# A memset behind each early gather, replaced by a wait for the gather two in front

## The chip, the cores and the metric

The kernel runs on one core of a Trainium2 chip. Its time is the device time of one execution, in microseconds; of the kernel before there are three runs, and their median is 1738.09 us (1730.94 to 1742.48). One further execution was taken with the hardware profiler, and all rows below are of that one.

A core has five engines with one instruction stream each: TensorE (PE, its weight loads PEld), VectorE (DVE), ScalarE (ACT), GpSimd (POOL) and SyncE (SP). They meet only at semaphores. Sixteen DMA engines move data; SP and POOL each feed a queue of their own.

## The reference

One layer of message passing on a graph with 100000 nodes of 64 numbers and 25000 edges:

```python
h = relu(layernorm(x))
edge_in_f = concat(h[src], h[dst], edge_attr)
edge_in_r = concat(h[dst], h[src], edge_attr)
agg = segment_sum(mlp_f(edge_in_f), dst) + segment_sum(mlp_r(edge_in_r), src)
out = x + h + mlp_n(concat(agg, h))
```

Each `mlp` is two matrix products with a relu between them; messages have 128 numbers. All is in 32-bit floats.

## The kernel before, in words

Three passes follow each other.

*First node pass.* The nodes go in 98 windows of 1024. SP loads a window of x (L384), DVE and ACT normalise it, PE multiplies it by the part of the first node weights that meets h, and SP stores the rows, 512 KB a window, to a table in memory (L390). Helper functions whose names end in `begin` are this pass.

*Edge pass.* The edges go in 98 batches of 256, two to a pair, so 49 pairs. For each batch the rows of x at both ends of its edges are needed: four tiles of 128 rows of 64 numbers, each fetched by an indirect DMA that POOL issues (L505, a "gather": 128 rows of 256 bytes, 32 KB). They are normalised, multiplied, and the messages of equal targets are joined; POOL then adds them to the table with four indirect DMAs (L523, a "scatter"). A batch's scatters wait for the landing of the batch before (L514 or L516). Behind such waits stands `sem_inc`, which counts up a semaphore that nobody waits for; wait and count are one instruction of POOL's own sequencer, and the indirect DMA behind it is another.

*Second node pass.* The table is read back, window by window, the node network is finished, and the result is stored.

**The early gathers.** The rows for the even batches of all 49 pairs are fetched during the first node pass into `got_even`, 196 gathers (4 per pair); those of the odd batches of the first four pairs into `got_odd`, 16 gathers. The other odd gathers, 180, are issued later, between the scatters. The early ones stand on POOL in a plain sequence, after a short setup: for each of the first four pairs four odd and four even, then only even ones. The first of all waits for the row numbers (`s_first`, counted up by DVE at L876); it carries that wait itself. Behind each even gather stands a memset of a tile that nothing reads (`idle`, 128 x 512, L550), which waits for the memset before it. All even gathers count up one semaphore, `s_got_even`, by 16 each when they land.

DVE waits for all of them at once (L1063) after the first node pass; its next instruction (L1066) and all of the edge pass on DVE stand behind that wait. POOL's scatters stand behind the last early gather.

Of the kernel before, what the change touches and what calls it, by code (L numbers as in the profile page):

```python
# [28 lines left out]
P = 128  # L29
# [31 lines left out]
def run(eng, count, loops, behind, body):  # L61


    done = 0
    for begin, end, unroll in loops:
        assert begin % unroll == 0 and end % unroll == 0
        for n in range(done, begin):
            body(Step(count, n))
        with eng.Fori(0, (end - begin) // unroll) as turn:
            turn = eng.snap(turn)  # L70
            for n in range(unroll):
                body(Step(count, n, begin, unroll, turn))
        done = end
    for n in range(done, count + behind):
        body(Step(count, n))


def gnn_layer(nc, x, src, dst, edge_attr, W1_f, b1_f, W2_f, b2_f, W1_r, b1_r, W2_r, b2_r, Wn1, bn1, Wn2, bn2, out):
# [7 lines left out]
    KB = 2 * JT  # L86
    NT = -(-E // (P * JT)) * JT
    NB = NT // JT
    PAIRS = NB // 2
    TB = NT // 2  # L90
    TAIL = E - (NT - 1) * P
    RING = 4
    assert NB % 2 == 0 and 0 < TAIL < P and TB < P

    SPARE = N
# [20 lines left out]
    with ExitStack() as ctx:  # L116
        def sb(name, shape, dt=F32):
            return ctx.enter_context(nc.sbuf_tensor(name, shape, dt))

        def sem(name):  # L120
            return ctx.enter_context(nc.semaphore(name))

        def sems(name):
            return [sem(f"{name}{s}") for s in range(2)]
# [30 lines left out]
        def two(name, shape, dt=F32):  # L155
            return [sb(f"{name}{s}", [P] + shape, dt) for s in range(2)]
# [4 lines left out]
        gather_first = sb("gather_first", [P, NB * KB], I32)  # L161
        gather_at = [sb(f"gather_at{p}", [P, KB], I32) for p in range(RING)]
        got_even = sb("got_even", [P, PAIRS, KB * D])
        got_odd = [sb(f"got_odd{p}", [P, 1, KB * D]) for p in range(RING)]
        sums = two("sums", [KB])
# [28 lines left out]
        nstd = two("nstd", [G])  # L194
        nh = [sb(f"nh{p}", [P, G, D]) for p in range(NRING)]
        nxh = [sb(f"nxh{p}", [P, G, D]) for p in range(NRING - 1)]
        idle = sb("idle", [P, 512])
        kept_more = sb("kept_more", [P, MORE, G * D])
        nturned = two("nturned", [G // 2 * P])
        nhidden = two("nhidden", [G * P])  # L200
# [19 lines left out]
        s_others = sems("others_in_")  # L220
        s_gat = [sem(f"gather_at_ready{p}") for p in range(RING)]
        s_got = [sem(f"rows_gathered{p}") for p in range(RING)]
        s_got_even = sem("even_rows_gathered")
        s_first = sem("gather_first_ready")
        s_paused = sem("pause_done")
        s_sums = sems("sums_ready")
        s_centred = sems("centred_ready")
        s_squared = sems("squares_ready")
# [20 lines left out]
        s_gathers_begun = sem("gathers_begun")  # L249
# [39 lines left out]
        def first(i):  # L289
            return isinstance(i, int) and i == 0  # L290
# [195 lines left out]
        @block.gpsimd  # L486
        def _(pool):

            for end in (SRC, DST):
                pool.iota(ends_int[:, end, :, :], pattern=[[0, 2], [1, P]], base=PAD + end * P,  # L490
                          channel_multiplier=0).then_inc(s_padded, 1)
            pool.iota(spare[:, :], pattern=[[P, KB]], base=SPARE, channel_multiplier=1,
                      allow_small_or_imprecise_dtypes=True).then_inc(s_const, 1)
            pool.memset(ident[:, :], 0.0).then_inc(s_filled, 1)
            pool.memset(earlier[:, :], 1.0).then_inc(s_filled, 1)
            pool.wait_ge(s_filled, 2)
            pool.affine_select(out=ident[:, :], in_=ident[:, :], compare_op=ALU.not_equal, fill=1.0, base=0,
                               pattern=[[-1, P]], channel_multiplier=1).then_inc(s_const, 1)
            tail = earlier[:, (KB - 1) * P:]
            pool.affine_select(out=tail, in_=tail, compare_op=ALU.is_gt, fill=0.0, base=0,  # L500
                               pattern=[[-1, P]], channel_multiplier=1).then_inc(s_const, 1)

            def gather(to, numbers, landed, tiles=range(KB)):
                for k in tiles:
                    pool.indirect_dma_start(to[:, k * D:(k + 1) * D], None, x,  # L505
                                            bass.IndirectOffsetOnAxis(ap=numbers[:, k:k + 1], axis=0)
                                            ).then_inc(landed, 16)

            def scatter(i, s):
                pool.wait_ge(s_sat[s], i + 1)  # L510
                pool.wait_ge(s_send[s], i + 1)

                if s == 1:
                    pool.wait_ge(s_added[0], 16 * KB * (i + 1))  # L514
                elif not first(i):
                    pool.wait_ge(s_added[1], 16 * KB * i)  # L516
                else:
                    pool.wait_ge(s_table0, 16)
                    for q in range(2):
                        pool.wait_ge(b_stored[q], 16 * (NW // 2))  # L520
                pool.sem_inc(s_scatters_begun, 1)
                for k in range(KB):
                    pool.indirect_dma_start(table, bass.IndirectOffsetOnAxis(ap=scatter_at[s][:, k:k + 1], axis=0),  # L523
                                            to_send[s][:, k, :], None, compute_op=ALU.add).then_inc(s_added[s], 16)

            def gather_odd(w):


                pair = w.of(2, 2 * RING)[0]
                turn, place = w.of(2 * RING, 2 * RING)  # L530
                place //= 2
                half = w.n % 2
                if half == 0:
                    pool.wait_ge(s_gat[place], turn)
                    pool.wait_ge(s_centred[1], pair - RING + 1)
                    pool.sem_inc(s_gathers_begun, 1)
                gather(got_odd[place][:, 0, :], gather_at[place], s_got[place],
                       range(half * JT, (half + 1) * JT))


            pool.wait_ge(s_first, 1)
            pauses = 0
            for i in range(PAIRS):
                if i < RING:
                    gather(got_odd[i][:, 0, :], gather_first[:, (2 * i + 1) * KB:(2 * i + 2) * KB], s_got[i])
                for k in range(KB):
                    gather(got_even[:, i, :], gather_first[:, 2 * i * KB:(2 * i + 1) * KB], s_got_even, [k])
                    if pauses:
                        pool.wait_ge(s_paused, pauses)
                    pool.memset(idle[:, :], 0.0).then_inc(s_paused, 1)  # L550
                    pauses += 1

            def batch(w):
                w.do(scatter)
                if w.there(2 * RING):
                    gather_odd(w)

            run(pool, NB, [(8, 88, 2 * RING)], 0, batch)
# [302 lines left out]
        def _(dve):  # L861
# [198 lines left out]

            dve.wait_ge(s_setup_ev, 6)
            dve.wait_ge(s_const, 6)
            dve.wait_ge(s_got_even, 16 * KB * PAIRS)  # L1063
            for s in range(2):
                dve.wait_ge(b_rstd[s], NW // 2)
            dve.scalar_tensor_tensor(out=all_sums[:, :, :], in0=all_sums[:, :, :], scalar=-1.0 / D,  # L1066
# [46 lines left out]
```

## Time and profile before

| | |
|---|---|
| median of three runs | 1738.09 us |
| the profiled execution | 1738.6 us, of which its span is 1736.9 |
| busy PE / DVE / ACT / POOL | 1324.7 / 971.1 / 945.3 / 1153.9 us |
| L523 POOL, 392 scatters | 647.5 us busy, 1652 ns each |
| L505 POOL, 196 gathers to `got_even` | 202.0 us busy, 1030 ns each |
| L505 POOL, 16 early gathers to `got_odd` | begun from 14.6 to 55.5 us |
| L550 POOL, 196 memsets | 538 to 552 ns each, the last at 378.9 us |
| mean granted clock of TensorE | 0.819 |

A span runs from the first to the last instruction. Busy time of POOL in an indirect DMA is the time in which it makes the transfer's descriptors, not the time of the transfer. The chain of waits follows the work that ended last back from the end of the span, at each step to what released it.

### The profile page before, as it was taken

Reading aid. Unit: us, or ns where it says so; the run is one execution under the profiler, and the core shown is the slowest. Engines: PE = TensorE matmul, PEld = TensorE weight load, DVE = VectorE, ACT = ScalarE, POOL = GpSimd, SP = SyncE. Lnnn points to the kernel's source line nnn. Section 1 sums busy time; section 2 is a strip of 40 time slices with the busy share of each in tenths; the row PEclk is TensorE's granted clock in tenths of the full one; section 3 lists DMA queues with packets and bytes.
Section 4 is the critical chain, followed back from the end, with each engine's and each line's share of the span. In section 5 each row is a group of like instructions: output and inputs, shape, how many; then the busy total and the mean of one; then the engine's idle time right before and its main releaser. Section 6 shows DMA issues by size and latency. Waiting matters only on the chain.

```text
span 1736.9 us, 28959 instructions
## 1 busy us (share of the span) xinstructions
PE 1324.7 (76%) x7070; PEld 1002.9 (58%) x7070; DVE 971.1 (56%) x2902; ACT 945.3 (54%) x2256; POOL 1153.9 (66%) x991
## 2 busy tenths in 40 slices
PE   4898985018777767777777878887877783999998
PEld 4777774006566555565565656665655563666665
DVE  6999994016656556656666666665566560222222
ACT  4888885016444544444444445554445442777776
POOL 6899988965877878778778887787777763000000
PEclk9999998558777877777777777777777776999999
DMA  6899996004555555555555555555555545999998
GB/s 188 303 316 311 312 313 223 20 15 101 106 100 95 106 98 104 107 97 104 109 96 104 107 99 101 108 93 101 97 94 99 96 63 147 344 355 356 338 344 291
DMA packets 240646, 284.90 MB, mean 164 GB/s; under 512 B 53394, under 2 KB 155424, under 8 KB 240620
## 3 DMA queue, kind: packets, MB, share of 16 engines
q1 hardware_dynamic: 171628, 246.06, 42.7%
q0 software_dynamic: 68992, 38.59, 19.5%
q14 instruction: 21, 0.17, 0.0%
q8 instruction: 5, 0.08, 0.0%
HBM read 164.72 MB, written 119.82 MB: 164 GB/s over the span
## 4 chain that ended last, share of the span: by engine, by line
POOL 50%; issue 21%; DMA 17%; PE 6%; DVE 4%; SPq 1%; ACT 0%; POOLq 0%; DVEq 0%; ACTq 0%
POOL table L523 25%; POOL got_even L505 12%; DMA out_x<-nout 11%; POOL got_odd L505 7%; POOL idle L550 6%; DMA table<-to_send,scatter_at 5%; PE bank L804 2%; DVE nout L1085 2%; PE bank L780 1%; PE bank L778 1%; PE bank L791 1%; DVE same L932 1%; PE bank L829 1%; DMA same<-table 1%; PE bank L840 0%
## 5 line engine op out<-in xcount | busy, mean ns | idle before, releaser
L523 POOL DMA_INDIRECT table<-to_send,scatter_at x392 | 647.5, 1652 | 197.0 <-issue 128.4
L804 PEld LDWEIGHTS bank<-message,same 128*128 128x128 f32 x1960 | 293.1, 238 | 46.1 <-issue 42.7
L804 PE MATMUL bank<-message,same 128*128 128x128 f32 x1960 | 314.9, 330 | 3.2 <-DVE message L963 3.2
L766 PE MATMUL bank<-ident,h_ends 128*128 128x128 f32 x196 | 54.6, 374 | 312.7 <-DVE h_ends L972 312.6
L606 ACT ACTIVATE nh<-nx,all_sums,all_rstd 128x64 f32<-128x64 f32 x784 | 280.4, 433 | 0.0
L505 POOL DMA_INDIRECT got_even<-in_x,gather_first x196 | 202.0, 1030 | 36.2 <-issue 36.2
L736 PE MATMUL bank<-wn_h,nturned 128*128 128x256 f32 x784 | 195.5, 393 | 29.7 <-ACT nhidden L644 24.6
L766 PEld LDWEIGHTS bank<-ident,h_ends 128*128 128x128 f32 x196 | 28.7, 187 | 325.3 <-issue 325.2
L505 POOL DMA_INDIRECT got_odd<-in_x,gather_at x180 | 179.9, 999 | 54.9 <-issue 54.9
L957 DVE TENSOR_TENSOR scatter_at<-moved,ids 128x4 int32<-128x4 f32 x98 | 15.9, 163 | 325.0 <-DMA table<-to_send,scatter_at 312.0
L736 PEld LDWEIGHTS bank<-wn_h,nturned 128*128 128x128 f32 x784 | 142.6, 192 | 65.2 <-issue 33.2
L780 PE MATMUL bank<-turned_edge,w_edge 64*128 64x256 f32 x392 | 177.6, 542 | 0.0
L778 PE MATMUL bank<-turned,w_ends 128*128 128x256 f32 x392 | 174.6, 537 | 1.0 <-ACT turned_edge L578 1.0
L944 DVE CUSTOM_DVE_ANT_0 junk<-same,earlier 128x128 bf16<-128x128 f32 (+3 forms) x392 | 168.8, 487 | 0.0
L674 ACT ACTIVATE nhidden<-bank,bn_col 128x512 f32<-128x512 f32 x196 | 124.0, 684 | 77.3 <-PE bank L829 77.3
L791 PE MATMUL bank<-w2n,hidden 128*128 128x128 f32 x784 | 149.8, 355 | 0.0
L585 ACT ACTIVATE hidden<-bank,b 128x256 f32<-128x256 f32 x196 | 82.1, 470 | 123.6 <-PE bank L780 108.7
L932 DVE TENSOR_SCALAR same<-others,ids 128x128 f32<-128x128 int32 (+3 forms) x392 | 141.7, 423 | 11.7 <-DVE ids L924 7.8
L829 PE MATMUL bank<-ident,same 128*128 128x128 f32 x784 | 108.4, 282 | 43.4 <-DMA same<-table 41.6
L791 PEld LDWEIGHTS bank<-w2n,hidden 128*128 128x128 f32 x784 | 140.1, 267 | 1.8
L566 ACT ACTIVATE squares<-centred 128x256 f32<-128x256 f32 x98 | 40.5, 413 | 178.5 <-DVE centred L916 155.4
L829 PEld LDWEIGHTS bank<-ident,same 128*128 128x128 f32 x784 | 85.5, 142 | 84.0 <-issue 51.4
(77 smaller groups left out, 1976.0 us busy)
## 6 DMA issues: line engine op xcount, KB each, us to landing
nx<-in_x SPq DMA_DIRECT2D x194, 256.0 KB
table<-nhidden SPq DMA_DIRECT2D x97, 512.0 KB
same<-table SPq DMA_DIRECT2D x97, 512.0 KB, 5.5
others<-numbers SPq DMA_DIRECT2D x196, 128.0 KB
out_x<-nout SPq DMA_DIRECT2D x97, 256.0 KB, 4.4
out_x<-nxh SPq DMA_DIRECT2D x63, 256.0 KB
nx<-out_x SPq DMA_DIRECT2D x63, 256.0 KB, 4.8
table<-to_send,scatter_at POOLq DMA_INDIRECT x392
```

The lines of the kernel that those rows point to most:

```text
L505: pool.indirect_dma_start(to[:, k * D:(k + 1) * D], None, x, bass.IndirectOffsetOnAxis(ap=numbers[:, k:k + 1], axis=0)).then_inc(landed, 16)
L523: pool.indirect_dma_start(table, bass.IndirectOffsetOnAxis(ap=scatter_at[s][:, k:k + 1], axis=0), to_send[s][:, k, :], None, compute_op=AL ...
L606: last = act.activation(nh[s][:, g, :], nx[place][:, g, :], ACT.Relu, bias=all_sums[:, at, g:g + 1].rearrange("p a g -> p (a g)"), scale=a ...
L674: act.activation(nhidden[s][:, odd * 512:odd * 512 + 512], bank[2 + 2 * s + odd][:, :], ACT.Relu, bias=bn1_col[:, 0:1]).then_inc(n_hidden[ ...
L736: last = pe.matmul(bank[2 + 2 * s + half][:, c:c + 2 * M], nturned[s][:, q * P:(q + 1) * P], wn1_h[:, :, :].rearrange("p a m -> p (a m)"), ...
L778: pe.matmul(bank[2 + s][:, c:c + JT * P], w1_ends[:, end, :], turned[s][:, 0:JT * P], start=True, stop=False)
L780: last = pe.matmul(bank[2 + s][:, c:c + JT * P], w1_edge[:, end, :], turned_edge[s][:, :], start=False, stop=True)
L791: last = pe.matmul(bank[4 + s][:, k * M:(k + 1) * M], hidden[s][:, end, j * P:(j + 1) * P], w2n[:, end, :], start=True, stop=True)
L804: last = pe.matmul(bank[6 + s][:, k * M:(k + 1) * M], same[s][:, o, k * P:(k + 1) * P], message[s][:, o, :], start=(o == k), stop=(o == KB ...
L829: last = pe.transpose(bank[2 + 2 * s + odd][:, q * P:(q + 1) * P], ntab[place][:, g * M:(g + 1) * M], ident[:, :])
L932: last = dve.tensor_scalar(same[s][:, o, 0:w], row[:, 0:w], ids[s][:, o:o + 1], None, ALU.is_equal)
L944: last = dve.tensor_tensor_reduce(junk[s][:, k, 0:w], same[s][:, k, 0:w], earlier[:, KB * P - w:], 1.0, 0.0, ALU.mult, ALU.add, before[s][ ...
```

## The change

The memset and its semaphore go, and so does the tile. The even gathers count up two semaphores in turn. In front of each even gather but the first two, POOL waits until the gather that used the same semaphore last, the one two in front, has landed, and counts up `s_gathers_begun`, a semaphore that nobody waits for. DVE waits for both semaphores' full counts where it waited for one. The four odd gathers of each of the first four pairs stay as they were.

```diff
--- before.py
+++ after.py
@@ -90,6 +90,7 @@
     TB = NT // 2
     TAIL = E - (NT - 1) * P
     RING = 4
+    FLIGHT = 2
     assert NB % 2 == 0 and 0 < TAIL < P and TB < P
 
     SPARE = N
@@ -194,7 +195,6 @@
         nstd = two("nstd", [G])
         nh = [sb(f"nh{p}", [P, G, D]) for p in range(NRING)]
         nxh = [sb(f"nxh{p}", [P, G, D]) for p in range(NRING - 1)]
-        idle = sb("idle", [P, 512])
         kept_more = sb("kept_more", [P, MORE, G * D])
         nturned = two("nturned", [G // 2 * P])
         nhidden = two("nhidden", [G * P])
@@ -220,9 +220,8 @@
         s_others = sems("others_in_")
         s_gat = [sem(f"gather_at_ready{p}") for p in range(RING)]
         s_got = [sem(f"rows_gathered{p}") for p in range(RING)]
-        s_got_even = sem("even_rows_gathered")
+        s_got_even = [sem(f"even_rows_gathered{p}") for p in range(FLIGHT)]
         s_first = sem("gather_first_ready")
-        s_paused = sem("pause_done")
         s_sums = sems("sums_ready")
         s_centred = sems("centred_ready")
         s_squared = sems("squares_ready")
@@ -539,16 +538,18 @@
 
 
             pool.wait_ge(s_first, 1)
-            pauses = 0
+            begun = 0
             for i in range(PAIRS):
                 if i < RING:
                     gather(got_odd[i][:, 0, :], gather_first[:, (2 * i + 1) * KB:(2 * i + 2) * KB], s_got[i])
                 for k in range(KB):
-                    gather(got_even[:, i, :], gather_first[:, 2 * i * KB:(2 * i + 1) * KB], s_got_even, [k])
-                    if pauses:
-                        pool.wait_ge(s_paused, pauses)
-                    pool.memset(idle[:, :], 0.0).then_inc(s_paused, 1)
-                    pauses += 1
+                    flown, lane = divmod(begun, FLIGHT)
+                    if flown:
+                        pool.wait_ge(s_got_even[lane], 16 * flown)
+                        pool.sem_inc(s_gathers_begun, 1)
+                    gather(got_even[:, i, :], gather_first[:, 2 * i * KB:(2 * i + 1) * KB], s_got_even[lane],
+                           [k])
+                    begun += 1
 
             def batch(w):
                 w.do(scatter)
@@ -1060,7 +1061,8 @@
 
             dve.wait_ge(s_setup_ev, 6)
             dve.wait_ge(s_const, 6)
-            dve.wait_ge(s_got_even, 16 * KB * PAIRS)
+            for lane in range(FLIGHT):
+                dve.wait_ge(s_got_even[lane], 16 * len(range(lane, KB * PAIRS, FLIGHT)))
             for s in range(2):
                 dve.wait_ge(b_rstd[s], NW // 2)
             dve.scalar_tensor_tensor(out=all_sums[:, :, :], in0=all_sums[:, :, :], scalar=-1.0 / D,
```

POOL's stream at the start of the early gathers, before. In it `got_odd` and `got_even` are the tiles that the gathers fill, `idle` is the memset's; what a row waits for stands in brackets.

```order
L505 DMA got_odd<-in_x,gather_first 128x64 [waits gather_first_ready]
L505 DMA got_odd<-in_x,gather_first 128x64 x3
L505 DMA got_even<-in_x,gather_first 128x64
L550 MEMSET idle 128x512
L505 DMA got_even<-in_x,gather_first 128x64
L550 MEMSET idle 128x512 [waits pause_done]
```

The same place now (the line numbers are lower by one from here on; the sequencer's own instruction that holds wait and count is not shown as a row, and the wait is told on the row behind it):

```order
L504 DMA got_odd<-in_x,gather_first 128x64 [waits gather_first_ready]
L504 DMA got_odd<-in_x,gather_first 128x64 x3
L504 DMA got_even<-in_x,gather_first 128x64 x2
L504 DMA got_even<-in_x,gather_first 128x64 [waits even_rows_gathered0]
L504 DMA got_even<-in_x,gather_first 128x64 [waits even_rows_gathered1]
L504 DMA got_odd<-in_x,gather_first 128x64 x4
```

No gather changed its place among the gathers; where a memset stood behind each, a wait stands in front.

## Rows read from the trace of the kernel before

**Rows 1.** The page's chain that ended last: shares by engine, then by line.

```profile
POOL 50%; issue 21%; DMA 17%; PE 6%; DVE 4%; SPq 1%; ACT 0%; POOLq 0%; DVEq 0%; ACTq 0%
POOL table L523 25%; POOL got_even L505 12%; DMA out_x<-nout 11%; POOL got_odd L505 7%; POOL idle L550 6%; DMA table<-to_send,scatter_at 5%; PE bank L804 2%; DVE nout L1085 2%; PE bank L780 1%; PE bank L778 1%; PE bank L791 1%; DVE same L932 1%; PE bank L829 1%; DMA same<-table 1%; PE bank L840 0%
```

**Rows 2.** Stretches: length, busy PE, PEld, DVE, ACT, POOL, granted clock, DMA share, GB/s.

```profile
63.50:286.00 222.50, 200.49 (x997) 160.68 (x996) 213.42 (x410) 193.25 (x413) 198.56 (x247) 1.00 0.90 307
286.00:379.00 93.00, 1.73 (x8) 1.17 (x7) 0.00 (x0) 2.15 (x4) 83.89 (x114) 0.53 0.16 46
379.00:405.00 26.00, 19.27 (x65) 13.22 (x66) 14.86 (x54) 13.06 (x40) 0.49 (x2) 0.53 0.12 34
```

**Rows 3.** Waits from 0 to 420 us: who for whom, total, times, longest.

```profile
DVE all_sums L1066 <- DMA got_even<-in_x,gather_first: 97.9, 1, 97.9
```

**Rows 4.** POOL's timeline from 100 us: start, duration, instruction, idle time before it.

```profile
102.33 1.29 POOL L505 DMA_INDIRECT got_even<-in_x,gather_first  x1 [0.16 <-issue]
103.62 0.54 POOL L550 MEMSET idle<- 128x512 f32 x1
104.32 1.09 POOL L505 DMA_INDIRECT got_even<-in_x,gather_first  x1 [0.16 <-issue]
...
106.11 0.96 POOL L505 DMA_INDIRECT got_even<-in_x,gather_first  x1 [0.16 <-issue]
...
107.76 1.11 POOL L505 DMA_INDIRECT got_even<-in_x,gather_first  x1 [0.16 <-issue]
```

**Rows 5.** POOL's timeline from 297 us, two gathers that follow each other.

```profile
298.33 0.96 POOL L505 DMA_INDIRECT got_even<-in_x,gather_first  x1 [0.16 <-issue]
...
299.99 0.96 POOL L505 DMA_INDIRECT got_even<-in_x,gather_first  x1 [0.16 <-issue]
```

**Rows 6.** DMA issues from 63.5 to 286 us, the line of the even gathers.

```profile
got_even<-in_x,gather_first POOLq DMA_INDIRECT x124
```

**Rows 7.** Timeline of DVE and POOL at the first gathers.

```profile
13.91 0.37 DVE L876 TENSOR_SCALAR gather_first<-ends_col 128x392 int32<-128x392 f32 x1
...
14.56 1.14 POOL L505 DMA_INDIRECT got_odd<-in_x,gather_first  x1 [11.59 <-DVE gather_first L876]
...
17.29 0.95 POOL L505 DMA_INDIRECT got_odd<-in_x,gather_first  x1 [0.30 <-issue]
```

**Rows 8.** Chain of waits at the last early gather: start, length, what.

```profile
377.95 2.36 DMA got_even<-in_x,gather_first
```

**Rows 9.** DMA from 14 to 103.2 us: POOL's queue (packets, MB, share), its gathers.

```profile
q0 software_dynamic: 1728, 1.77, 8.3%
...
got_even<-in_x,gather_first POOLq DMA_INDIRECT x39
...
got_odd<-in_x,gather_first POOLq DMA_INDIRECT x16
```

**Rows 10.** Queues, 103.2:104.9 (all there is), then 104.9:105.9, 107.55:108.65, 110.2:111.0 (POOL's).

```profile
q1 hardware_dynamic: 170, 0.48, 83.3%
...
q0 software_dynamic: 32, 0.03, 9.3%
...
q0 software_dynamic: 62, 0.06, 17.2%
...
q0 software_dynamic: 30, 0.03, 11.0%
```

**Rows 11.** POOL's queue from 379.5 to 380.1 us.

```profile
q0 software_dynamic: 32, 0.03, 22.6%
```

**Rows 12.** Chain of waits at a scatter near 611 us, and at the first.

```profile
606.47 4.63 DMA table<-to_send,scatter_at
...
611.12 0.02 POOLq L521
611.14 0.79 issue
...
404.13 0.82 issue
```

## What the change will do to the time

> **What bounds the kernel now.** I read the chain of waits first. POOL holds half of it; the scatters of the edge pass (L523) take 25% and the early gathers (L505 with the memset L550) take 12 + 7 + 6% [rows 1]. The table of windows then shows where the early gathers matter. From 63.5 to 286 us every engine is at work and the DMA engines are 90% busy; from 286 to 379 POOL alone works and DMA falls to 16% [rows 2]. In that second stretch DVE sits for 97.9 us at L1066 until the last even gather has landed [rows 3], and nothing of the edge pass starts before. So the end of the gather train sets the end of the kernel, one for one: each microsecond that the last landing moves, the end moves. How fast the stage beside it runs is of no account, since that stage is done some 90 us earlier.
>
> **The train now.** POOL begins a gather (0.96 to 1.29 us), then the memset (0.54), with 0.16 idle in front of the next gather; it waits for no landing. One turn takes 1.65 to 1.99 us beside the other engines' work [rows 4] and 1.66 when alone [rows 5]. The first 32 gathers (four odd, four even, four times over) are begun by 63.5 us. Of the other 180, all even, 124 are begun from 63.5 to 286 [rows 6]: 222.5 / 124 = 1.79 us each. The other 56 follow at 1.66.
>
> **What is removed.** 196 memsets of 0.54 us with their 0.16. Alone, gathers follow each other at 0.95 + 0.30 = 1.25 us, as the odd ones at the start do [rows 7]. That would be 180 x (1.79 - 1.25), up to 97 us, if no wait took the memset's place.
>
> **What is added.** In front of each even gather but the first two, a wait for the landing of the one two in front, and an increment of a counter behind it, both in one instruction of POOL's sequencer. Behind it on POOL stand all later gathers, and then the scatters. The pace becomes the larger of the issue pace, 1.25, and (landing time + time to wake) / 2. Both terms have rows.
>
> *Landing, quiet.* The last gather begins at 377.95 and has landed 2.36 us later [rows 8].
>
> *Landing beside the other work.* No row gives it directly, but the packets of POOL's DMA queue do. A gather is 32 packets: from 14 to 103.2 us 39 + 16 = 55 gathers were begun and 1728 = 54 x 32 packets went [rows 9]. So all but the gather that began at 102.33 were through. Its packets do not go from 103.2 to 104.9, where the queue has no row at all; 32 go from 104.9 to 105.9. Those of the gathers begun at 104.32 and 106.11 go together from 107.55 to 108.65 (62 recorded), those of the one begun at 107.76 from 110.2 to 111.0 (30 recorded) [rows 4, 10]. With the pair's first one put at 108.1, from begin to last packet this is 3.57, 3.8, 2.54 and 3.24, mean 3.29 us. The quiet gather's packets are through by 380.1 at the latest [rows 11] and its landing is seen at 380.31, so I add 0.25 (an estimate): 3.54 us.
>
> *Waking.* The scatters have the same form, a wait and an increment in one sequencer instruction, then the indirect DMA. At 611.10 a landing ends such a wait, the sequencer's L521 runs from 611.12, and then 0.79 us pass until the DMA begins at 611.93; for the first scatter of all it is 0.82 [rows 12]. From landing to begin that is 0.83, of which I take 0.81. The nearest other row is the very first gather, which carries its wait itself: DVE ends at 13.91 + 0.37 = 14.28 and POOL begins at 14.56, 0.28 us [rows 7]. So waking costs between 0.28 and 0.82. I take 0.81, because the changed gathers have the scatter's form; no row shows a gather behind such an instruction with POOL idle. With the memset POOL was still at work while its sequencer ran ahead, so this time was hidden; with POOL idle at the wait it is bare.
>
> The Trainium skill, page "DMA: Bandwidth & Descriptors", section "Anatomy of one DMA — SWDGE (gpsimd) path", puts the sequencer's dispatch at about 50 ns. Going by that, waking would be some 0.28 + 0.05 = 0.33 us, an estimate, and the sum below would give about 1733; the 0.79 of the scatters speaks against it.
>
> **The sum.** Quiet pace: (2.36 + 0.81) / 2 = 1.59, against 1.66: a small gain. Busy pace by the mean: (3.54 + 0.81) / 2 = 2.18, against 1.79: a loss. It should be somewhat more, because the packets go in bursts about 2.65 us apart [rows 10], and a gather that just misses one waits for the next; a gather whose two predecessors both missed takes 5.3 / 2 = 2.65. Between 2.18 and 2.65 I take 2.3, nearer the mean, since the rows show both short and long landings. Then 222.5 / 2.3 = 96 gathers are begun by 286, and 84 are left. The last begins at 286 + 83 x 1.59 = 418, lands at 420.4 instead of 380.3: +40 us. The first 32 cost about nothing: of an even quartet the third gather starts 4.35 us behind the first in place of 3.4, and the fourth and the next odd one win back 0.45 each.
>
> DVE's two waits in place of one hit a time when DVE idles: nothing. The edge pass is the same code. TensorE's granted clock is 0.53 both in the quiet stretch and in the 26 us behind it [rows 2], near the lower level (1.2 GHz) already, so a longer pause takes nothing more there. The profiled execution took 1738.6 us, 0.5 above the median of the runs shown (1738.1). 1738.6 + 40 = 1778.6, that is **1778** against the median.
>
> **Ends.** With waking 0.81 and the plain mean, 2.18: 102 begun by 286, 78 left, last landing 410.8, +30: 1769. With 2.65: 84 begun, 96 left, 439, +59: 1798.
>
> **Rivals.**
> 1. *Waking is cheap* (0.28). Busy (3.54 + 0.28) / 2 = 1.91, 116 begun; the 64 others at 1.32; last landing 371.5, -9: 1730, no change that can be told. For: the first gather's row. Against: 0.79 and 0.82 at the form that is really used. Chance 0.11.
> 2. *Faster: the long landing is of the train's own making.* If two gathers in flight no longer queue behind each other, the landing beside other work falls to the quiet 2.36, and the pace is 1.59 throughout: 63.5 + 179 x 1.59 + 2.36 = 350.5, -30: 1709. It decides as soon as the busy landing is under 2 x 1.79 - 0.81 = 2.77 us. For: one of four landings is 2.54. Against: by these landings about two were in flight already (3.54 / 1.79), and from 103.2 to 104.9 one gather waits alone [rows 9, 10]. Chance 0.07. The same page of the Trainium skill gives one DMA of this path as 2.0 us plus bytes / 436e3, about 2.08 us for 32 KB, an estimate that would make it 1682; the quiet row (2.36) agrees roughly, the busy ones do not.
> 3. *The waits never close* (each landing is in time): the issue pace of 1.25 holds, the train ends with the stage beside it near 290, about 1648. The quiet landing alone, 2.36 against 2 x 1.25 = 2.5, would allow it only if waking cost nothing. Chance 0.02.
> 4. *Locked to the bursts* (2.65 throughout the busy stretch): 1798, as above. For: the next gather begins 0.81 us behind a landing and its packets need a lead of at least 1.55 us (begun at 377.95, none before 379.5) [rows 8, 11], which together with the bursts' length of about 1 us is more than a burst's distance. Against: short landings exist. Chance 0.12.
>
> **Numbers.** The forecast itself has 0.68. A measurement of this kernel tells about 1% (17 us) from no change. Slower by over 1%: forecast and rival 4, 0.80. Within 1%: rival 1, 0.11. Faster: rivals 2 and 3, 0.09. The range leaves out rivals 1 to 3, two in ten, and holds forecast and lock with their bounds: a busy pace of 2.0, with landings a little shorter, is +16 by the same sum, 1755, and a waking time of 0.7 in place of 0.81 would take some 9 us from any case, so 1748 below; above, a busy pace of 2.85, the lock with a further miss now and then, is +69, of which I take nearly all: 1806.
>
> **What would show it.** DVE's wait at L1066 (now L1068) grows from 97.9 to about 138 us. From 63.5 to 286 us 96 gathers are begun in place of 124 (84 to 102). In the quiet stretch they come in pairs, 3.17 us per pair. In front of most gathers POOL idles with the landing of a got_even gather as releaser, with about 0.8 us between landing and begin. No memset at L550. The stretch from the last landing to the end keeps its 1356 us. I would be wrong if gathers begin 0.3 us behind a landing (rival 1), or if busy landings come near 2.4 us (rival 2).

## The result, and the profile after

The changed kernel takes 1800.93 us (median of 4 runs, 1798.3 to 1804.91), the kernel before 1740.28 on the same chips (4 runs): a ratio of 1.036, with a 95% interval of 1.0313 to 1.0406. It is slower by some 61 us. The forecast was 1778, the range 1748 to 1806.

The stretches of the profiled execution, with the columns of [rows 2]:

```profile
63.50:286.00 222.50, 201.06 (x994) 161.53 (x995) 216.93 (x416) 194.28 (x416) 94.70 (x87) 0.99 0.89 302
286.00:379.00 93.00, 6.52 (x32) 4.97 (x30) 0.89 (x2) 5.93 (x13) 50.93 (x54) 0.55 0.19 57
379.00:443.00 64.00, 0.00 (x0) 0.00 (x0) 0.00 (x0) 0.00 (x0) 38.45 (x41) 0.50 0.09 21
443.00:470.00 27.00, 18.27 (x58) 12.24 (x59) 14.77 (x53) 12.08 (x36) 1.47 (x2) 0.51 0.12 34
```

From 63.5 to 286 us the other engines and the DMA engines are as busy as before. But POOL is busy for 94.7 us in place of 198.6, and the stretch in which it works alone has grown by some 64 us. Its gathers in the first stretch, against 124 [rows 6]:

```profile
got_even<-in_x,gather_first POOLq DMA_INDIRECT x87
```

The waits from 0 to 480 us (who for whom, total, times, longest):

```profile
POOL got_even L504 <- DMA got_even<-in_x,gather_first: 159.9, 87, 3.3
DVE all_sums L1068 <- DMA got_even<-in_x,gather_first: 158.8, 1, 158.8
```

DVE's wait for the last even gather was 97.9 [rows 3] and is 158.8, 60.9 more, about the difference of the medians. The landing that ends it (chain of waits):

```profile
443.85 2.34 DMA got_even<-in_x,gather_first
```

It comes at 446.2 in place of 380.3, 65.9 later. That is 5 us more than DVE's wait has grown, since DVE also comes to the wait 5 us later: from 14 to 63.5 us PE did 163 matmuls in place of 181. There the change lets up to eight gathers go without a pause; that this is the reason is not shown by a run of its own. POOL itself now waits 159.9 us for landings. How, its timeline from 98 us shows (start, duration, instruction, idle before it and its releaser):

```profile
98.52 1.48 POOL L504 DMA_INDIRECT got_even<-in_x,gather_first  x1 [2.70 <-DMA got_even<-in_x,gather_first]
100.31 0.95 POOL L504 DMA_INDIRECT got_even<-in_x,gather_first  x1 [0.30 <-issue]
104.04 1.21 POOL L504 DMA_INDIRECT got_even<-in_x,gather_first  x1 [2.78 <-DMA got_even<-in_x,gather_first]
105.56 0.95 POOL L504 DMA_INDIRECT got_even<-in_x,gather_first  x1 [0.30 <-issue]
109.40 1.30 POOL L504 DMA_INDIRECT got_even<-in_x,gather_first  x1 [2.89 <-DMA got_even<-in_x,gather_first]
```

Where [rows 4] had a gather every 1.65 to 1.99 us, here two begin close together and then nothing for 2.8 us; from pair to pair it is 5.52 and 5.36 us. The chain of waits at the same place (start, length, what; POOLq is POOL's sequencer):

```profile
98.52 4.72 DMA got_even<-in_x,gather_first
...
103.27 0.02 POOLq L549
103.28 0.55 issue
103.84 0.02 POOLq L549
...
104.04 4.56 DMA got_even<-in_x,gather_first
```

The first of a pair lands 4.72 and 4.56 us after its begin, not 3.54. POOL's sequencer takes the landing at 103.27, has the next gather ready and is at the next wait at 103.84, and the gather begins at 104.04, 0.79 us behind the landing. The wait at 103.84 is for the second gather of the pair and is over at once: that one, begun at 100.31, had landed too, at most 3.53 us after its begin. The packets show both in one burst. The DMA queues from 102 to 103.5 us (POOL's), from 103.5 to 107.4 (all there is) and from 107.4 to 109 (POOL's), as packets, MB, share:

```profile
q0 software_dynamic: 64, 0.07, 13.4%
...
q1 hardware_dynamic: 418, 1.10, 93.1%
...
q0 software_dynamic: 64, 0.07, 13.6%
```

64 packets are two gathers; then POOL's queue has none for 3.9 us, although a gather begins at 104.04. SP's stores of windows begin at 98.87, 101.47, 104.10, 106.83 and 109.56 in this trace, some 2.7 us apart, so a pair takes two windows. Alone it looks so:

```profile
349.04 2.31 DMA got_even<-in_x,gather_first
...
351.38 0.75 issue
352.14 2.41 DMA got_even<-in_x,gather_first
```

From 349.04 to 352.14 two gathers begin in 3.10 us (3.17 forecast).

### The profile page after: what moved, and what is told of

It reads as the page before. It is cut to its first block, busy times and chain, and to the rows that moved or that the text cites. A ratio compares the mean times of both kernels' runs of the same rounds, so it can differ in the third digit from the quotient of the medians.

```text
span 1800.7 us, 28958 instructions
## 1 busy us (share of the span) xinstructions
PE 1320.4 (73%) x7070; PEld 1000.7 (56%) x7070; DVE 972.4 (54%) x2902; ACT 946.0 (53%) x2256; POOL 1047.9 (58%) x795
## 4 chain that ended last, share of the span: by engine, by line
POOL 37%; DMA 32%; issue 24%; PE 3%; DVE 2%; SPq 1%; POOLq 1%; ACT 0%; DVEq 0%; ACTq 0%
POOL table L522 28%; DMA got_even<-in_x,gather_first 16%; DMA out_x<-nout 11%; POOL got_odd L504 8%; DMA table<-to_send,scatter_at 4%; DVE nout L1087 2%; POOL got_even L504 1%; PE bank L830 1%; PE bank L841 1%; PE bank L805 1%; DMA same<-table 0%; PE bank L781 0%; PE bank L779 0%; DMA ends_int<-in_dst 0%; PE bank L851 0%
## 5 line engine op out<-in xcount | busy, mean ns | idle before, releaser
L504 POOL DMA_INDIRECT got_even<-in_x,gather_first x196 | 200.5, 1023 | 207.2 <-DMA got_even<-in_x,gather_first 159.9
L805 PEld LDWEIGHTS bank<-message,same 128*128 128x128 f32 x1960 | 289.0, 235 | 45.6 <-issue 42.0
L805 PE MATMUL bank<-message,same 128*128 128x128 f32 x1960 | 310.9, 327 | 3.4 <-DVE message L964 3.4
```

Of the source, the lines that this page charges most:

```text
L504: pool.indirect_dma_start(to[:, k * D:(k + 1) * D], None, x, bass.IndirectOffsetOnAxis(ap=numbers[:, k:k + 1], axis=0)).then_inc(landed, 16)
L805: last = pe.matmul(bank[6 + s][:, k * M:(k + 1) * M], same[s][:, o, k * P:(k + 1) * P], message[s][:, o, :], start=(o == k), stop=(o == KB ...
```

## The experiments

**The theories.** A: gathers begin 0.79 us behind a landing, miss the next burst of packets, and land in the one after it, so that two gathers go per two bursts (5.3 us) while the node pass runs. B: a landing is some 3.5 us whatever the phase, and the pace is the mean of landing and waking, shared by the gathers in flight. C: the long landing is made by the gathers themselves.

**1 to 3. Three in flight, four, and no pause at all.** In the first two, `FLIGHT = 2` is 3 or 4. The third:

```diff
-                    if flown:
-                        pool.wait_ge(s_got_even[lane], 16 * flown)
-                        pool.sem_inc(s_gathers_begun, 1)
```

> Three gathers in flight in place of two. Theory A (locked to the bursts: gathers begin 0.79 us behind a landing, miss the next burst and land in the one after it): three per 5.3 us in the busy stretch, pace 1.77, some 126 begun from 63.5 to 286; then the issue pace of 1.25; last landing about 355, 25 us sooner than before: 1713. Rival B (landing is 3.5 us whatever the phase): (3.54 + 0.79) / 3 = 1.44, some 154 begun, last landing about 322, 1680. Rival C (the landing is of the train's own making and grows with the gathers in flight): pace stays near 2.5, 1780 or so.

> Four gathers in flight. Theory A: four per 5.3 us, about the issue pace beside the other work (1.07 + 0.30 = 1.37), some 162 begun by 286, last landing 310, 1668. Rival B: issue pace too, the same 1668. Rival C: pace 2 or more, over 1750.

> Neither memset nor wait: every early gather is issued as soon as POOL has issued the one before. Theories A and B: issue pace 1.37 beside the other work, 1.25 alone, last landing 310, 1668, and the first node pass is not slowed. Rival C (a pause is needed, since gathers that pile up hold each other or the node pass's stores up): the node pass ends over 10 us later or POOL stalls in its gathers, 1720 or more.

Measured: 1908.06 (ratio 1.0955, 1.0935 to 1.0975), 1911.39 (1.0974, 1.0951 to 1.0996) and 1901.93 (1.0937, 1.0911 to 1.0964). The times of A and B fail by more than 190 us. C's outcome for the run without pause came (the node pass ends over 10 us later, 1720 or more), but the size it gave with three in flight, 1780, is too small by 128, and its reason, long landings, is not what happens. Stretches of the run without pause, with the columns of [rows 2]:

```profile
63.50:286.00 222.50, 30.88 (x84) 23.11 (x84) 18.96 (x35) 15.93 (x35) 168.03 (x174) 0.55 0.20 50
...
300.00:545.00 245.00, 208.28 (x1020) 166.83 (x1018) 219.37 (x424) 199.69 (x426) 0.00 (x0) 0.97 0.79 271
```

The gathers do run at the issue pace: POOL begins 174 in these 222.5 us, 1.28 us each. It is the node pass beside them that stands still, with PE busy for 31 us in place of 200; it mostly takes place from 300 to 545, when POOL has finished. So these runs do not decide between A and B: both took the node pass for granted, and without it there are no bursts to lock to. The stores of its windows in the same stretch, in the run without pause:

```profile
table<-nhidden SPq DMA_DIRECT2D x7, 512.0 KB
got_even<-in_x,gather_first POOLq DMA_INDIRECT x174
```

and with three in flight:

```profile
table<-nhidden SPq DMA_DIRECT2D x6, 512.0 KB
```

Before, it was 84 stores. The gate of three hardly bites: with the node pass standing still landings are short, POOL waits 16 us for them in all (159.9 in the change), and the pace is that of no wait at all. What the other engines wait for is not a busy engine, nor the DMA engines, which are 20% busy. Waits of the run without pause from 64 to 288 us (`remote` is a release that the view can't place):

```profile
ACT nturned L635 <- remote: 177.8, 6, 31.4
```

One such wait, from PE's timeline and from the chain of waits:

```profile
68.94 1.00 PE L723 MATMUL bank<-ident,nh 128*128 128x128 f32 x4
...
65.97 18.63 another core or an unknown queue
...
84.63 11.19 issue
95.82 0.04 ACT nturned L635
```

ACT's copy needs the transposes of PE that end at 69.94, and PE's next work begins at 97.44; the copy begins at 95.82, 26 us later. DVE and PE go on only behind ACT.

SP's timeline in the same run:

```profile
65.47 0.36 SPq L389 DMA_DIRECT2D table<-nhidden  x1
69.87 0.70 SPq L383 DMA_DIRECT2D nx<-in_x  x1
97.56 0.35 SPq L389 DMA_DIRECT2D table<-nhidden  x1
102.78 0.69 SPq L383 DMA_DIRECT2D nx<-in_x  x1
```

The same in the kernel before:

```profile
104.27 0.35 SPq L390 DMA_DIRECT2D table<-nhidden  x1
104.82 0.34 SPq L384 DMA_DIRECT2D nx<-in_x  x1
```

A store and the load behind it, 0.55 us apart before, are 4.4 and 5.2 us apart; the load's issue takes SP 0.70 us in place of 0.34 (the store's 0.36, as before); and the next store comes after 32 us. The trace also holds the register instructions of SP's sequencer, which the views leave out: the plain move in front of such a load (L383) takes 0.70 us, in the kernel before (L384) 0.03. So the sequencers of SP and ACT are held up while POOL issues gathers at this pace, and the other two engines stand behind ACT. What holds the sequencers is not shown by any row; the runs below say from which pace on.

**4. The gather carries its wait.** As the change, without the count between wait and gather:

```diff
                         pool.wait_ge(s_got_even[lane], 16 * flown)
-                        pool.sem_inc(s_gathers_begun, 1)
```

> Two in flight as in the change, but no counting up between wait and gather, so that the gather itself carries the wait. If waking then costs 0.28 us as at the very first gather: quiet pace (2.36 + 0.28) / 2 = 1.32 in place of 1.58, and in the busy stretch 0.5 us earlier is enough for part of the gathers to reach the next burst, pace 1.9 or so; last landing about 371, 1730. If waking stays at 0.79 (the sequencer's work for a gather is not done ahead of the wait): as the change, 1800. If waking is 0.28 but the lock holds (pace 2.65 while busy): last landing 414, 1772.

Measured: 1753.94, ratio 1.009 (1.0065 to 1.0115), between the stated cases. The chain of waits in the busy stretch:

```profile
99.76 3.71 DMA got_even<-in_x,gather_first
103.47 0.26 issue
103.73 3.09 DMA got_even<-in_x,gather_first
106.81 0.26 issue
107.07 4.20 DMA got_even<-in_x,gather_first
```

And where POOL works alone:

```profile
329.26 2.47 DMA got_even<-in_x,gather_first
331.72 0.26 issue
331.98 2.40 DMA got_even<-in_x,gather_first
```

Waking is 0.26 us, as at the first gather of all [rows 7], and alone the pair takes 2.72 us. In the busy stretch the gathers begun are

```profile
got_even<-in_x,gather_first POOLq DMA_INDIRECT x106
```

222.5 / 106 = 2.10 us each against 222.5 / 87 = 2.56. Waking fell by 0.53; by the plain mean that is 0.27 per gather, measured is 0.46. The rest is in the landings that a gather is waited for: 3.71, 3.09 and 4.20 here, 4.72 and 4.56 in the change. A begin 0.53 us sooner gets the train out of the lock in these rows (3.97 and 3.34 us from one to the next), as A says and B, with its one landing for every phase, does not.

**5. The wait and the memset together.** As the change, with the memset put back behind each even gather, and its own wait on the memset before it (the lines that make the tile and the semaphore are left out here):

```diff
+                    if begun:
+                        pool.wait_ge(s_paused, begun)
+                    pool.memset(idle[:, :], 0.0).then_inc(s_paused, 1)
                     begun += 1
```

> The change's wait, and the memset behind each even gather kept as before. Theory A (the wait costs: two gathers per 5.3 us while busy, and the memset is hidden in POOL's idle time): busy stretch as in the change, some 85 gathers begun from 63.5 to 286; alone the memset's pace holds, 1.66 in place of 1.62; last landing about 448, 1803. Rival (it is the memset's absence that costs, since POOL then disturbs the other engines as in the run without memset or wait): the node pass or the train gets back to before's, 1740 to 1750.

Measured: 1813.33 (one execution), with

```profile
got_even<-in_x,gather_first POOLq DMA_INDIRECT x90
```

from 63.5 to 286. The last early gather begins at 443.9 us, in the change at 443.8. So, for the train, the wait alone makes the loss; taking the memset away neither adds to it nor, behind such a wait, saves anything. The 12 us by which this execution is longer than the change lie behind the train and are not explained.

**6. A later start.** As the change, with a memset of 128 x 768 between each wait and its gather (tile and semaphore again left out):

```diff
                         pool.sem_inc(s_gathers_begun, 1)
+                        if flown + lane > 1:
+                            pool.wait_ge(s_paused, begun - FLIGHT)
+                        pool.memset(idle[:, :], 0.0).then_inc(s_paused, 1)
```

> As the change, but between a landing and the gather that waits for it stands a memset of 128 x 768, about 0.8 us, which makes waking 1.2 us or so in place of 0.79. Theory A (locked: the gathers miss the burst by some 0.7 us anyway and idle until the next one): the busy pace stays at 2.6, 83 to 88 gathers begun from 63.5 to 286 (87 in the change); alone the pace rises from 1.62 to about 1.8. Last landing about 457, 1812. Rival B (no lock: pace is the mean of landing and waking over two): busy pace 2.58 + 0.2 = 2.8, 79 begun; last landing about 468, 1823.

Measured: 1833.9 (one execution). The chain:

```profile
95.93 4.42 DMA got_even<-in_x,gather_first
...
101.39 4.24 DMA got_even<-in_x,gather_first
```

and the count from 63.5 to 286:

```profile
got_even<-in_x,gather_first POOLq DMA_INDIRECT x86
```

Waking is 1.04 us, since the sequencer readies the gather during the memset; that is 0.25 more than in the change, less than I meant to add. In the busy stretch it costs one gather of 87, where B's mean asks for four (2.56 + 0.125 = 2.68, 83): the landing gets shorter by what the begin gets later, and from 95.93 to 101.39 a pair takes 5.46 us and the next one 5.27, as in the change (5.52 and 5.36). That is what A says. The test is a weak one, because the step was small. The time came out above both cases for a simple reason: alone, POOL needs memset and gather twice per pair, 1.87 us each with the gaps, and that is more than landing and waking. The last gather begins at 475.0, 31 us later than in the change, and most of that is lost in the quiet stretch.

**7. No memset where POOL works alone.** As before, but

```diff
-                    if pauses:
-                        pool.wait_ge(s_paused, pauses)
-                    pool.memset(idle[:, :], 0.0).then_inc(s_paused, 1)
-                    pauses += 1
+                    if i < PAIRS - 12:
+                        if pauses:
+                            pool.wait_ge(s_paused, pauses)
+                        pool.memset(idle[:, :], 0.0).then_inc(s_paused, 1)
+                        pauses += 1
```

> As before, but the last 12 pairs' 48 gathers, which begin when the first node pass is over, have no memset behind them. If the harm of gathers without a break is done to the other engines' work alone, there is none here: pace 1.25 in place of 1.66 for 48 gathers, 19.7 us less, 1720. If gathers without a break hold each other up, no gain: 1740.

Measured: 1720.08, ratio 0.9886 (0.9838 to 0.9934). Its timeline past the node pass:

```profile
321.06 0.95 POOL L505 DMA_INDIRECT got_even<-in_x,gather_first  x1 [0.30 <-issue]
322.31 0.95 POOL L505 DMA_INDIRECT got_even<-in_x,gather_first  x1 [0.30 <-issue]
```

DVE's wait for the last gather:

```profile
DVE all_sums L1067 <- DMA got_even<-in_x,gather_first: 76.3, 1, 76.3
```

1.25 us per gather, DVE's wait is 21.6 us shorter, and the time 20. Alone, gathers without a break do each other no harm, so C is out as far as it speaks of the gathers themselves. This version beats both kernels, the one before by some 1%.

**8 to 10. How much of a pause.** Run 8 is the kernel before with a memset of 128 x 64 (`idle` is made smaller). Runs 9 and 10 are run 7 with 128 x 384, and with 128 x 256 and only the last 9 pairs without memset.

> As before, with a memset of 128 x 64 (about 0.14 us) in place of 128 x 512 behind each gather, so that gathers begin at nearly the pace of the run without memset or wait (0.96 + 0.14 + 0.16 = 1.26 alone, 1.37 beside other work). Theory P (what starves the other engines is the pace of the gathers): as without memset or wait, about 1900. Theory Q (any other instruction between two gathers lets the other engines' sequencers through): the node pass runs as before, the train ends about 310 to 320, 1675.

> As the run whose last 48 gathers have no memset, with a memset of 128 x 384 (about 0.42 us) in place of 128 x 512 behind the others. Pace alone 1.54, beside other work about 1.67. If the harm to the other engines only begins at paces nearer 1.44: 133 gathers begun from 63.5 to 286, last landing about 346, 34 us sooner than before: 1706. If the harm grows evenly from 1.79 downwards: the node pass ends 20 us or more later and most of this is lost, 1720 to 1740.

> As before, with a memset of 128 x 256 (about 0.30 us), and none behind the last 9 pairs' 36 gathers. Pace alone 1.42, beside other work about 1.55. Without harm: 143 begun from 63.5 to 286, last landing about 333, 1693. If the harm sets in above a pace of 1.44 already: the node pass ends after 330 and holds the edge pass up, 1750 to 1850.

Run 8: 1869.64, ratio 1.0761 (1.068 to 1.0842). From 63.5 to 286 us:

```profile
table<-nhidden SPq DMA_DIRECT2D x18, 512.0 KB
...
got_even<-in_x,gather_first POOLq DMA_INDIRECT x155
```

Another instruction between two gathers does not help; the node pass is held up at 222.5 / 155 = 1.44 us per gather, a little less than at 1.28. Run 9: 1720.23, 0.9872 (0.9812 to 0.9932), no gain on run 7, against its expectation of 1706: it began 124 gathers from 63.5 to 286, where 133 were expected and the kernel before has 124 too, so the shorter memset did not quicken the train there. Run 10: 1715.94, 0.9894 (0.9813 to 0.9976; its four runs lie between 1696 and 1734), with

```profile
table<-nhidden SPq DMA_DIRECT2D x81, 512.0 KB
...
got_even<-in_x,gather_first POOLq DMA_INDIRECT x137
```

so that at 222.5 / 137 = 1.62 us the node pass is hardly held up (81 stores; 84 before). Runs 7, 9 and 10 can't be told apart.

## Why the prediction was right, and where not

The mechanism was right and the time lies in the range, but not near the forecast: 1778 gives two thirds of the loss, and 1801 is next to rival 4's 1798. That the range held it is owed to that rival, which had a chance of 0.12 and set the upper end.

*What bounds the kernel*: right. The end of the gather train moved from 380.3 to 446.2, +65.9. From there to the end of the span it is 1354.5 us, 1356.6 before.

*The two terms of the pace*: right. Waking is 0.79 in the change (0.81 taken), and 0.26 when the gather carries its wait (run 4), so the instruction between wait and gather is what makes it dear. The quiet pair took 3.10 us at the rows above (3.17).

The Trainium skill, page "DMA: Bandwidth & Descriptors", section "Anatomy of one DMA — SWDGE (gpsimd) path", gives about 50 ns for the sequencer's dispatch. This trace does not agree for an indirect gather: from one wait to the next, with one gather readied between them, POOL's sequencer took 0.55 us (103.28 to 103.84).

*The busy pace*: the term that was too small. I took 2.3 us, near the plain mean of 2.18; measured is 222.5 / 87 = 2.56, nearly rival 4's 2.65. The landings I averaged were those of a train that did not wait, with begins at all phases of the bursts, and the mean lets each of the two places turn by itself. In the change both gathers of a pair land in one burst, so only the first one's landing counts: 4.6 us, not 3.54, and 4.6 + 0.79 = 5.4 a pair. The second one's is 3.53 at most, but its place stays empty until POOL has begun the first of the next pair. Over the whole stretch the pace is 2.56 and not 2.7, because the train falls out of step now and then. That rival's argument (waking and lead together are longer than the way to the next burst) was sound, and should have set the number. Runs 4 and 6 agree with it. By 286 us 30 + 87 gathers were begun instead of 32 + 96: 11 more were left, at 1.6 us 18 us of the 26 by which the train's end lies behind the forecast's 420.4. The rest is the pace behind 286, (446.2 - 286) / 95 = 1.69 in place of 1.6.

*What is removed*: the memset's time came back nowhere, as said, because the wait takes its place (run 5). But the sentence on what would be won without any wait, up to 97 us, and rival 3 with its 1648, were wrong: without wait or memset the kernel takes 1902, not 1648. I had taken the node pass beside the train to be of no account. It is so only as long as the train's pace leaves the other engines alone.

*Rivals 1 and 2*: out. Waking is not 0.28 behind such an instruction, and the landings that are waited for beside the node pass are 4.6 us, far from 2.36, though the gathers were fewer.

*DVE's two waits, the edge pass, the clock*: nothing to be seen, as said. The granted clock behind the longer pause is 0.51 (0.53 before).

## What to carry to other kernels

A landing time read from a stream that runs freely is a mean over phases. Where the packets go in bursts, a stream that waits for its own landings can fall into step with them: its transfers land together, and each turn pays the whole way to the next burst but one. A wait that the indirect DMA carries itself cost 0.26 us between landing and begin, one in an instruction in front of it 0.79. A pause that looks like waste may protect what runs beside it: here it could go where nothing else runs (20 us), and with the pause gone everywhere the kernel took 161 us more.

## What was not expected of the hardware

While POOL issues gathers of 128 rows every 1.28 us, all the other engines nearly stand still: 7 of 84 window stores in 222.5 us, with the DMA engines 20% busy, and SP needing 0.70 us to issue a load that takes 0.34. At 1.44 us it was 18 stores, at 1.62 us 81, at 1.79 us 84. The Trainium skill, page "DMA: Bandwidth & Descriptors", section "SWDGE vs HWDGE vs iDMA", says of transfers that SP issues that they are immune to the interference between DVE and GpSimd over descriptor writes; here SP's own loads take twice as long to issue, so whatever acts is something else. Which resource the sequencers share with POOL's gathers stays open: no experiment separated the making of the descriptors from the handing of instructions to POOL. The scatters of the edge pass, begun 1.85 to 2.07 us apart with gaps of 0.30, are slower than the paces that hurt.
